# Decayed attention: from all pairs of 512 tokens to a scan over two chunks of 256 with a state per head

## What is computed

```python
sl = slopes[:, None, None]                                   # one slope per head
mask = where(t[:, None] >= t[None, :], exp(-sl * (t[:, None] - t[None, :])), 0)
q_dec, k_dec, blk_dec = exp(-slopes*(t+1)), exp(-slopes*(chunk-1-t)), exp(-slopes*chunk)
def step(kv, inp):                                           # chunk = 128 in the reference
    qi, ki, vi = inp
    scores = einsum('bhtd,bhsd->bhts', qi, ki) * mask
    o = einsum('bhts,bhsd->bhtd', scores, vi) + einsum('bhtd,bhde->bhte', qi * q_dec, kv)
    kv = blk_dec * kv + einsum('bhtd,bhte->bhde', ki * k_dec, vi)
    return kv, o
```

## Time and profile before

| | us |
|---|---|
| time before, median of 3 runs | 3385.95 (3382.43 to 3387.8) |
| the profiled execution: its time | 3384.29 |
| its span | 3382.5 |
| the decayed layer within it, first load issued to last normalization | 1451.6 to 2209.0 |
| mean granted PE clock | 0.926 of full speed |

### The profile page before, as it was taken

How to read it: one execution, slowest core, us unless ns; L and a number is a source line. 1 busy time by engine, 2 the same in 40 slices (tenths; PEclk the granted TensorE clock), 3 DMA queues, 4 the chain that set the end, 5 groups by cost and what they waited for, 6 DMA issues and landing times. The chain is left out here.

```text
span 3382.5 us, 61649 instructions
## 1 busy us (share of the span) xinstructions
PE 2859.8 (85%) x16506; PEld 2062.8 (61%) x16507; DVE 2033.0 (60%) x3929; ACT 1337.5 (40%) x2815; POOL 965.4 (29%) x1303
## 2 busy tenths in 40 slices
PE   5998999989999958859999999868888888818992
PEld 4666666666666647747777777635544445417992
DVE  3666656566665568835666666566566566535664
ACT  3555554545545412222222222224444444424443
POOL 4334343343433211123333333210111111121225
PEclk8999999999999979979999999979888888868996
DMA  1101111011111021020000000031222211134225
GB/s 61 38 24 41 39 29 36 30 41 38 29 31 31 30 83 37 31 97 12 11 11 11 12 12 12 7 96 51 62 62 62 61 51 51 30 105 133 72 73 193
DMA packets 124632, 163.92 MB, mean 48 GB/s; under 512 B 19706, under 2 KB 87954, under 8 KB 123794
## 3 DMA queue, kind: packets, MB, share of 16 engines
q1 hardware_dynamic: 113300, 138.40, 13.9%
q0 software_dynamic: 6912, 18.96, 1.5%
q10 hardware_dynamic: 4224, 4.19, 0.4%
HBM read 87.73 MB, written 37.06 MB: 37 GB/s over the span
## 5 line engine op out<-in xcount | busy, mean ns | idle before, releaser
L1115 ACT ACTIVATE soft_probs<-soft_ps_s,soft_mx 128x512 f32<-128x512 f32 x512 | 347.9, 685 | 395.5 <-DVE soft_mx L1034 371.1
L1839 DVE TENSOR_REDUCE mla_mx<-mla_ps_s 128x1 f32<-128x512 f32 x512 | 334.2, 684 | 242.9 <-PE mla_ps_s L1699 225.3
L1034 DVE TENSOR_REDUCE soft_mx<-soft_ps_s 128x1 f32<-128x512 f32 x512 | 329.1, 684 | 236.9 <-PE soft_ps_s L944 224.3
L1942 ACT ACTIVATE mla_pt<-mla_ps_t 128x512 f32<-128x512 f32 x512 | 292.8, 600 | 397.5 <-PE mla_ps_t L1711 361.2
L944 PE MATMUL soft_ps_s<-soft_ks,soft_qs 128*128 128x512 f32 x1024 | 310.8, 423 | 10.3 <-ACT soft_probs L1115 10.3
L953 PE MATMUL soft_ps_p<-ident,soft_probs 128*128 128x128 f32 x2048 | 267.2, 273 | 12.6 <-issue 6.1
L953 PEld LDWEIGHTS soft_ps_p<-ident,soft_probs 128*128 128x128 f32 x2048 | 237.5, 141 | 47.5 <-issue 7.8
L944 PEld LDWEIGHTS soft_ps_s<-soft_ks,soft_qs 128*128 128x128 f32 x1024 | 171.6, 190 | 144.7 <-issue 59.2
L1044 DVE COPY soft_pt<-soft_ps_p 128x512 f32<-128x512 f32 x256 | 175.4, 685 | 137.3 <-PE soft_ps_p L953 134.6
L1699 PE MATMUL mla_ps_s<-mla_stack,mla_pad 128*128 128x512 f32 x512 | 236.0, 468 | 22.4 <-DVE mla_mx L1839 17.4
L962 PE MATMUL soft_ps_a<-soft_pt,soft_v 128*64 128x512 f32 x1024 | 251.9, 614 | 0.0
(11 more groups left out here) (337 smaller groups left out, 6580.7 us busy)
## 6 DMA issues: line engine op xcount, KB each, us to landing
soft_rrep<-inverse SPq DMA_DIRECT2D x128, 128.0 KB, 2.9
mla_pad<-mla_stack SPq DMA_DIRECT2D x256, 64.0 KB, 2.0
moe_xt<-by_expert SPq DMA_DIRECT2D x72, 129.0 KB, 2.1
soft_ks<-soft_ks SPq DMA_DIRECT2D x64, 128.0 KB, 2.3
raw<-in_L_ffn_w SPq DMA_DIRECT2D x16, 512.0 KB, 8.6
mla_stack<-mla_yh SPq DMA_DIRECT2D x128, 64.0 KB, 2.1
soft_xc<-in_L_attn_x SPq DMA_DIRECT2D x8, 512.0 KB, 4.1
soft_xb<-in_L_attn_x SPq DMA_DIRECT2D x8, 512.0 KB, 4.1
```

Source lines behind the costliest of these rows:

```text
L1034: op = vv.tensor_reduce(out=mx[:, h, t:t + 1], in_=ps_s[:, s_bank(4 * h + t), :], axis=AX.X, op=ALU.max, negate=True)
L1115: op = nc.scalar.activation(probs[:, h % 2, t, :], ps_s[:, s_bank(4 * h + t), :], ACT.Exp, bias=mx[:, h, t:t + 1], scale=1.0, accum_out=rs ...
L1839: op = vv.tensor_reduce(out=mx[:, a, t, s:s + 1], in_=ps_s[:, (16 * a + 4 * t + s) % S_BANKS, :], axis=AX.X, op=ALU.max, negate=True)
L1942: op = nc.scalar.activation(pt[:, t % 2, s, :], ps_t[:, s % 2, :], ACT.Exp, scale=KPH ** -0.5)
```

## The change

The layer gets a function of its own, `decay_attention`. It computes the scan with two chunks of 256 tokens. Scores are made only within a chunk (**S** g, c, n: group g of four heads, chunk c, three steps n of 512 columns each: two heads by 256 queries, four heads by 128 queries, two heads by 256 queries). **M** multiplies each by `near`. **A** g, c, q makes a pair of heads in one chunk: 256 and then 128 columns. What the second chunk takes from the first goes through a state: **VD** (DVE) weights v, **KV2** (PE) multiplies the rotated keys `kr` with it, **KH** (ACT) copies the state to `kv`, **IN** (PE) multiplies it with the queries into a bank `ps_i`, **TM** (DVE) weights that into `ot`, **OA** (DVE) adds A of the second chunk. The high part **HA** is on ACT, the low part **LA** on DVE in the first chunk and on POOL in the second. HI goes from ACT to POOL. Keys are turned over once (high and low stacked), and two transfers per key tile (**KD**, SP) make the swapped copy. VV (copy of v) goes from DVE to POOL. x for the residual (`xb`) is loaded by SP instead of copied by DVE (XB is gone). All of it is laid over 24 gaps per batch element by `put(gap, engine, steps)`; a step put below gap 24 is ahead.

```diff
-def attention(nc, const, x_in, x_out, w_q, w_kv, w_o, out_bias, rope_tab, decay_tab, softmax, name):
...
+def decay_attention(nc, const, x_in, x_out, w_q, w_kv, w_o, rope_tab, near_tab, from_tab, to_tab, name):
...
+CHUNK = 2 * P
+S_BANKS, RING, MISC = 2, 6, 3
+near = sb("near", [P, HEADS, CHUNK])
+from_end, to_start = sb("from_end", [P, 2, HEADS]), sb("to_start", [P, PAIRS, CHUNK])
+kr = sb("kr", [P, 2, KVW])
+vd = sb("vd", [P, 2, 2, GRP * HD])
+kv = sb("kv", [P, 2, GRP * HD])
+pt = sb("pt", [P, RING, SEQ])
+ot = sb("ot", [P, 2, CHUNK])
...
+blocks = [(0, 0), (1, 0), (0, 1), (1, 1), (2, 0), (3, 0), (2, 1), (3, 1)]
+ROUND, S0 = 3 * len(blocks), 13
+ENGINES = ("tensor", "vector", "scalar", "gpsimd", "sync")
+gaps, ahead_keys = {}, {eng: set() for eng in ENGINES}
+def put(at, eng, *keys):
+    assert 0 <= at < 2 * ROUND, (at, keys)
+    if at < ROUND:
+        ahead_keys[eng].update(keys)
+    gaps.setdefault((at % ROUND, eng), []).extend(keys)
+turned = lambda u: [("QT",) + u[1:] + (b,) for b in range(2)]
+def project(at, u, back):
+    put(at, "tensor", u)
+    put(at + 1, "vector", ("ROT",) + u, *([("VC", u[1])] if u[0] == "KV" else []))
+    put(at + 1, "gpsimd", *((n,) + u for n in ("Y0", "Y1", "HI", "LO")))
+    for key in (turned(u) if u[0] == "Q" else [("KT", u[1])]):
+        put(back, "tensor", key); put(back, "scalar", ("C",) + key)
+    if u[0] == "KV":
+        put(back, "sync", ("KD", u[1]))
+for k in range(KD):
+    put(0, "tensor", ("T", k)); put(0, "vector", ("XH", k), ("XL", k))
+for u, (at, back) in {("KV", 0): (2, 7), ("KV", 1): (3, 8), ("Q", 0, 0): (5, 9), ("Q", 0, 1): (7, 11), ("KV", 2): (9, 13), ("KV", 3): (11, 14),
+                      ("Q", 0, 2): (13, 16), ("Q", 0, 3): (15, 18), ("Q", 1, 0): (17, 20), ("Q", 1, 1): (19, 22), ("Q", 1, 2): (21, 24), ("Q", 1, 3): (22, 26)}.items():
+    project(at, u, back)
+put(10, "gpsimd", ("VV", 0)); put(15, "gpsimd", ("VV", 1))
+for g, at in enumerate((12, 14, 22, 25)):
+    put(at, "vector", ("VD", g)); put(at + 1, "tensor", ("KV2", g)); put(at + 1, "scalar", ("KH", g))
+for b, (g, c) in enumerate(blocks):
+    at = S0 + 3 * b
+    for n in range(3):
+        put(at + n, "tensor", ("S", g, c, n)); put(at + n + 1, "vector", ("M", g, c, n))
+    for q in range(2):
+        put(at + 3 + q, "tensor", ("A", g, c, q))
+    if c == 0:
+        put(at + 5, "scalar", ("HA", g, 0)); put(at + 5, "vector", ("LA", g, 0))
+    else:
+        put(at + 4, "tensor", ("IN", g)); put(at + 5, "vector", ("TM", g), ("OA", g))
+        put(at + 6, "scalar", ("HA", g, 1)); put(at + 6, "gpsimd", ("LA", g, 1))
+put(ROUND + 1, "sync", ("LX",)); put(ROUND + 2, "sync", ("LB",))
+for t, at in enumerate((34, 36, 41, 43)):
+    put(at, "tensor", ("W", t, 0)); put(at + 1, "tensor", ("W", t, 1))
+    put(at + 1, "vector", ("F", t), ("B", t), ("G", t)); put(at + 2, "gpsimd", ("EPS", t), ("RSTD", t))
+    put(at + 3, "vector", ("N", t)); put(at + 4, "sync", ("ST", t))
...
+turn = {"T": 0, "QT": 0, "KT": 0, "A": 1, "KV2": 1, "IN": 1, "W": 2, "S": 3, "Q": 4, "KV": 4}
+for g in range(ROUND):
+    gaps[g, "tensor"] = sorted(gaps.get((g, "tensor"), []), key=lambda k: -1 if k[0] == "W" and k[2] else turn[k[0]])
+    gaps[g, "vector"] = sorted(gaps.get((g, "vector"), []), key=lambda k: k[0] != "F")
+    gaps[g, "scalar"] = sorted(gaps.get((g, "scalar"), []), key=lambda k: k[0] != "HA")
...
+                    seq, prior = step_before(j, number[g, c, n], S_BANKS)
+                    pe.wait_ge(*dve_s.at(seq, "M", *prior))
+                    where = ps_s[:, number[g, c, n] % S_BANKS, :]
+                    if n == 1:
+                        tile, queries = 2 * c + 1, qs[:, GRP * g:GRP * g + GRP, CHUNK * c + P:CHUNK * c + CHUNK]
+                    else:
+                        h = GRP * g + n
+                        tile, queries = 2 * c, qs[:, h:h + 2, CHUNK * c:CHUNK * c + CHUNK]
+                    where = where.rearrange("p (h s) -> p h s", s=P if n == 1 else CHUNK)
+                    for b in range(2):
+                        last = nc.tensor.matmul(where, ks[:, b, g, P * tile:P * tile + P], queries, start=(b == 0), stop=(b == 1))
...
+                    pe.wait_ge(*dve_s.at(j, "M", g, c, 1 + q))
+                    at = CHUNK * q
+                    place = blocks.index((g, c)) % 2
+                    for s in range(2):
+                        last = nc.tensor.matmul(ps_a[HD * s:HD * s + HD, place, at:at + CHUNK], v[:, 1, 2 * c, HD * g:HD * g + HD],
+                                                weights_of(g, c, 2 * q)[:, s, :], start=True, stop=False)
+                    for s in range(2):
+                        last = nc.tensor.matmul(ps_a[HD * s:HD * s + HD, place, at + P:at + CHUNK], v[:, 1, 2 * c + 1, HD * g:HD * g + HD],
+                                                weights_of(g, c, 1)[:, 2 * q + s, :], start=False, stop=True)
...
+                    for t in range(2):
+                        for s in range(2):
+                            last = nc.tensor.matmul(m[HD * s:HD * s + HD, 0:GRP * HD], kr[:, t, HD * g:HD * g + HD], vd[:, g % 2, t, :], start=(t == 0), stop=(t == 1))
+                elif kind == "IN":
+                    g = key[1]
+                    pe.wait_ge(*act_s.at(j, "KH", g))
+                    pe.wait_ge(*(dve_s.at(j, "TM", g - 1) if g else dve_s.at(shift(j, -1), "TM", KVH - 1)))
+                    for q in range(2):
+                        for s in range(2):
+                            a = 2 * q + s
+                            last = nc.tensor.matmul(ps_i[HD * s:HD * s + HD, 0, CHUNK * q:CHUNK * q + CHUNK], kv[:, g % 2, HD * a:HD * a + HD],
+                                                    qs[:, GRP * g + a, CHUNK:2 * CHUNK].bitcast(F32), start=True, stop=True)
...
+                    heads = near[:, GRP * g:GRP * g + GRP, 0:P] if n == 1 else near[:, GRP * g + n:GRP * g + n + 2, :]
+                    op = vv.tensor_tensor(weights_of(g, c, n), ps_s[:, number[g, c, n] % S_BANKS, :].rearrange("p (h s) -> p h s", s=width), heads, ALU.mult)
...
+                    op = vv.tensor_tensor(ot[:, :, :].rearrange("p q s -> p (q s)"), ps_i[:, 0, :], to_start[:, 2 * g:2 * g + 2, :].rearrange("p q s -> p (q s)"), ALU.mult)
...
+        for n in (1, 0, 2):
+            hi_weights(n)
...
+                    op = nc.gpsimd.tensor_copy(stack[:, :, 0:HD].bitcast(F32R), rows)
```

More of the change, by code:

```diff
@@ L1173, in steps @@
                             op = nc.gpsimd.tensor_tensor(atl[:, p, :], ot[:, p % 2, :], ath[:, p, :].bitcast(F32), ALU.subtract)
+                        elif kind == "EPS":
+                            t = key[1]
+                            hold(pool, *dve_s.at(j, "G", t))
+                            op = nc.gpsimd.tensor_scalar(vare[:, t % 2, :], mv[:, t % 2, 1:2], EPS, None, ALU.add)
+                        elif kind == "RSTD":
+                            t = key[1]
+                            hold(pool, *pool_s.at(j, "EPS", t))
+                            hold(pool, *(dve_s.at(j, "N", t - 2) if t >= 2 else dve_s.at(shift(j, -1), "N", t + 2)))
+                            op = nc.gpsimd.tensor_tensor(rstd[:, t % 2, :], vare[:, t % 2, :], const["minus_half"][:, :], ALU.pow)
@@ L2430, in tables @@
     slopes = np.array([2.0 ** (-8.0 / HEADS * (i + 1)) for i in range(HEADS)], f).astype(np.float64)
-    dist = np.arange(SEQ)[None, :] - np.arange(P)[:, None]
-    decay = np.where(dist[:, None, :] >= 0, np.exp(-slopes[None, :, None] * np.maximum(dist, 0)[:, None, :]), 0.0).astype(f)
-    return {"rope0": pack(np.cos(ang), np.sin(ang)), "rope1": pack(np.cos(ang64), np.sin(ang64)), "decay": np.ascontiguousarray(decay)}
+    chunk = 2 * P
+    dist = np.arange(chunk)[None, :] - np.arange(P)[:, None]
+    near = np.where(dist[:, None, :] >= 0, np.exp(-slopes[None, :, None] * np.maximum(dist, 0)[:, None, :]), 0.0).astype(f)
+    left = chunk - 1 - np.arange(chunk).reshape(2, P).T
+    from_end = np.exp(-slopes[None, None, :] * left[:, :, None]).astype(f)
+    to_start = np.exp(-slopes.reshape(PAIRS, 2).T[:, :, None] * (np.arange(chunk) + 1.0))
+    to_start = np.repeat(to_start, HD, axis=0).astype(f)
+    return {"rope0": pack(np.cos(ang), np.sin(ang)), "rope1": pack(np.cos(ang64), np.sin(ang64)), "decay_near": near, "decay_from_end": from_end, "decay_to_start": to_start}
 def kernel(**inputs):
```

839 lines of the change are left out of this document (355 added, 484 removed).

## The result

The changed kernel took 3346.34 us (median of 4, 3337.12 to 3347.62), the kernel before 3385.75 beside it: a ratio of 0.9879 (95% interval 0.9859 to 0.9898), so 39.4 us less. Forecast were 3328 and 58 us less, within 3283 to 3364. The profiled execution took 3345.92, its span is 3344.2.

A forecast was written before the change was run, and what follows sets the result against it. PE was taken to bound the rounds. Rounds -31, start +2 and end -29.5 gave -58 us, so 3384.3 became 3326, and 3328 with the runs' median 1.7 higher; range 3283 to 3364.

The forecast's parts named there:

- the waits are those of the lists: PE's waits in a loop round, found gap by gap from PE's and DVE's lists laid side by side: sum 11.1 us.
- PE's work: PE's work in a loop round after the change: 69.2 us of products plus 2.4 for changes of form, 71.6; bounds 69 and 76.
- "thirty more" changes of form: PE changes form some 75 times a round against 45; at about 0.08 us each, thirty more cost 2.4.
- the 79.0 worked out for the old round: PE's work in a round of the kernel before, summed from start-to-start prices: 79.0 of 88.4 us.
- "waits and starts": The rest of the old 88.4 us round beside PE's work: 9.4 us of waits and starts after them.
- The round: One loop round of the changed layer: 82.7 us at full clock, taken as 84, 4.4 less; times 7, -31.
- KV2 and IN side by side: New PE products, their two output halves run side by side as in A: 0.92 us each, 7.4 a round.
- the rival of doubled cost: Clock falls in part or KV2 and IN cost double: rounds of 87 to 91 us, 3363 at 89; chance 0.22.
- The start: Layer's start before its loop, a rotation chain with 12 units ahead instead of 8: +2 us, bounds 0 and +10.
- The end: What is left of the last element after the loop: 43 us instead of 72.5, so -29.5.
- The clock: PE's granted clock in the rounds, taken as 0.98 from 0.97 to 0.99 before; under 0.95 would count as wrong.
- the slower rival: Clock stays at 0.86 as in latent attention: 94.4 us a round, +10.4 x 7 = +73, so 3401; chance 0.05.

The follow-up runs named there:

- e1: Changed kernel with DVE's order within each gap set to F, then M, then the rest; 3261.4 us, 0.9755 of the kernel before.
- e3: Changed kernel with F left at its planned place in DVE's gaps instead of in front; 3296.4 us, 0.9861 of the kernel before.
- e6: Changed kernel with one small awaited transfer ahead of the latent attention layer's first transfer; 3341.7 us, 0.9866 of the kernel before.
- e9: The same program as e1, run again in another session; 3267.4 us, 0.9769 of the kernel before.
- e10: e1 with LA, EPS and RSTD put first in POOL's gaps; 3246.7 us, 0.9708 of the kernel before.
- e11: e10 with S ahead of QT in T's gap and the first Q unit turned in gap 10, not 9; 3278.1 us, 0.9802 of the kernel before.

## Why the prediction was right, and by what it was off

- **PE bounds, and the waits are those of the lists:** right. There are six waits at A a round for M, as forecast, and they stand where they were put. The longest is behind T (2.13, forecast 2.2), then come 1.28 and 0.71 in the gaps of the two KV units (1.1, 1.0), 1.70 in gap 7 (1.7), 0.98 at gap 17 (0.85) and 1.20 near gap 19 (1.6). Beside them W waits 0.30 (0.5 at gap 18) and QT 0.72 for XL's bank (0.6). The wait at QT in gap 22 is 1.21, against 1.35. They sum to 10.2 in the round of 84.1, and the waits view gives the same on average, (32.0 + 4.8 + 2.9 + 1.2) / 4; forecast were 11.1. e1 shows that what stood ahead of M was the cause of the six.
- **PE's work was mis-sized, and this term makes most of the miss.** Taken from start to start without the waits, the round of 84.1 us at a granted 1.00 has 73.8 us of work; forecast were 71.6, of them 69.2 for the products and 2.4 for "thirty more" changes of form. The products were right where the form stays: units 17.4 (17.6), W 11.9 (11.4), KV2 and IN 7.6 (7.4), A 12.3 (12.0). The excess stands in the groups at which it changes, S 13.6 (11.8) and turned tiles 11.1 (9.0). PE's row of kinds changes 80 times in that round, and (73.8 - 69.2) / 80 = 0.06 us for each, no more than the 0.08 assumed. But I charged them only for the thirty that were added. Most of those of before were no part of the 79.0 worked out for the old round; they stood within its "waits and starts", 9.4, and when the waits were listed anew they were left out altogether: 80 x 0.0575 = 4.6 instead of 2.4, 2.2 us a round. That the excess belongs to the changes is argued from where it stands; no run varied their number alone.
- **The round:** 73.8 + 10.2 = 84.0 at full clock instead of 82.7, and on average 1.9 us for stretches at the lower level instead of 1.5. Together 85.9 instead of 84, and over 7 rounds some 14 us less gain. This is most of the miss of 18; the waits, 0.9 shorter than forecast, hid a part of it by luck.
- **KV2 and IN side by side, 0.92 each:** right (0.91, 0.96); the rival of doubled cost is out.
- **The start:** +5.5 instead of +2, within its bounds. The first ROT stands 14.3 after the first load instead of 13.4; that belongs to this execution, for in e3 and e6, whose start has the same code, it is 13.5 and 13.4 and the loop begins at 70.9 and 70.8, so +4.6. Of the rest, 1.85 is POOL standing still beside DVE's split of the output weights, and what is left is in the last six units, where ROT waits for PE three times (the chain took 55.3 from first to last ROT, 52 was forecast). The cost of the split in mid-chain had been taken for nothing because DVE had time for it; it was POOL that had not. The Trainium skill (SBUF — State Buffer, "SBUF: two separate sides") says that a DVE instruction with two inputs in SBUF and a GpSimd instruction that reads SBUF exclude each other for the whole instruction. The traces agree: POOL's two additions take 1.42 us beside no such instruction, 3.27 beside one of 2.28 and 5.32 beside two of 2.28 and 2.69. By that rule the +1.85 could have been forecast.
- **The end:** right, 42.6 against 43.
- **The clock:** granted at 0.96 to 1.00 in the rounds, as in the kernel before, with nine waits a round; the slower rival is out. The Trainium skill (TensorE: Matmul & The Clock Gate, "A second HAM failure mode: psum-queue depth-cycling") has it that brief idling between groups of matmuls can cost throughput by the clock. The runs agree in the direction: with the six waits at A gone a round at full clock takes 80.6 and the mean one 80.9 (e1) and 81.5 (e9), so the lower level costs 0.3 to 0.9 us a round instead of 1.9, and in e10 nothing in five rounds of six. But its size in this layer is 1.9 us a round and not the 10.4 of the slower rival.
- **The sum:** 58 forecast; 14 less in the rounds and 3.5 in the start give 40.5, and the layer became 40.9 shorter. (The chances as listed add up to 0.92 for faster and 0.05 for slower, where the summary has 0.91 and 0.06.)

## What to carry to other kernels

When engines run fixed lists, put what another engine waits for ahead in each stretch: one sorting key on DVE was worth nearly as much here (38 us) as the whole change of algorithm (41 us). Where buffers are given out in the order of a list, a step moved in it changes who waits for whom (e11). When a sum of prices is to be compared with a measured round, close the books on the old round first: what is left there must appear in the new sum too. Here that was some 2.6 us: 88.4 less 79.0 of work and less the 6.8 us that PE waits in that round (1696.4 to 1784.8), a part of it the clock's. And compare kernels only beside each other and by the layer that was changed; the same work took 3343 or 3386 us from one session to another.
